# Soft experts on one Trainium2 core: a third shift of the logits on TensorE, and the end of the stage reordered

## The reference, cut to what matters

```python
# x: 8 x 256 tokens, d = 128; n = 64 experts, p = 32 slots each (2048 slots)
logits = (einsum('tzd,ed->tze', x, phi_w) + phi_b).reshape(t, z, n, p)
D = softmax(logits, axis=3)            # over the slots of an expert
C = softmax(logits, axis=2)            # over the experts of a slot
X = clip(einsum('tznp,tzd->npd', D, x), -33000.0, 65000.0)
X = tanh((X - mean(X)) * rsqrt(var(X) + eps))
Y = einsum('npd,ndH->npH', X, expert_w) + expert_b
out = einsum('tznp,npH->tzH', C, Y)
```

## Time and profile before

| | us |
|---|---|
| median of 3 runs | 3192.12 (3189.71 to 3195.6) |
| the profiled execution | 3195.53 |
| its span, first to last instruction | 3193.8 |
| PE, DVE, ACT, POOL busy in the span | 91%, 68%, 52%, 35% |
| mean granted clock of PE | 0.882 |

### The profile page before, as it was taken

How to read it: one execution, slowest core, us unless ns; L and a number is a source line. 1 busy time by engine, 2 the same in 40 slices (tenths; PEclk the granted TensorE clock), 3 DMA queues, 4 the chain that set the end, 5 groups by cost and what they waited for, 6 DMA issues and landing times. The chain is left out here.

```text
span 3193.8 us, 59125 instructions
## 1 busy us (share of the span) xinstructions
PE 2901.8 (91%) x22942; PEld 1673.4 (52%) x22949; DVE 2175.2 (68%) x4849; ACT 1645.8 (52%) x3323; POOL 1120.1 (35%) x532
## 2 busy tenths in 40 slices
PE   8888899998999999898968898888889899998998
PEld 3333344343899999643444454444453344574547
DVE  5777635556677777767588886877861559926991
ACT  3554543443333333336466776776753557725761
POOL 1111130002100000100088787877840219912990
PEclk8999999999555555699979998999999899999999
DMA  5344323022000000030532222222202001250224
GB/s 155 93 103 105 90 83 113 7 88 87 4 4 4 4 4 4 2 109 13 199 100 88 80 90 80 87 84 80 90 27 99 5 1 79 93 198 1 93 107 183
DMA packets 113495, 234.37 MB, mean 73 GB/s; under 512 B 13760, under 2 KB 50752, under 8 KB 104768
## 3 DMA queue, kind: packets, MB, share of 16 engines
q1 hardware_dynamic: 113216, 230.59, 22.3%
HBM read 185.71 MB, written 44.83 MB: 72 GB/s over the span
## 5 line engine op out<-in xcount | busy, mean ns | idle before, releaser
L2723 DVE TENSOR_TENSOR_SCAN s_hh<-psum,s_dbu 128x512 f32<-128x512 f32 x384 | 447.3, 1206 | 76.0 <-ACT psum L2335 75.9
L1447 PE MATMUL psum<-h_ring,h_parts 128*128 128x4 f16 x12264 | 478.0, 168 | 0.6 <-DVE h_ring L1590 0.4
L2593 POOL TENSOR_TENSOR s_dbu<-s_du,s_bb 128x1024 f32<-128x1024 f32 x191 | 447.1, 2360 | 67.0 <-DVE s_hh L2723 56.3
L1447 PEld LDWEIGHTS psum<-h_ring,h_parts 128*128 128x128 f16 x12264 | 429.5, 106 | 48.8 <-DVE h_ring L1590 0.9
L1509 ACT ACTIVATE h_now<-psum 128x16 f32<-128x16 f32 x1024 | 188.4, 184 | 324.3 <-PE psum L1447 317.8
L2335 ACT ACTIVATE psum<-s_delta,s_decay 128x512 f32<-128x512 f32 x384 | 256.5, 685 | 108.4 <-DVE s_hh L2723 106.3
L2227 PEld LDWEIGHTS psum<-w_c,s_term 128*128 128x128 f32 x1536 | 202.2, 151 | 136.6 <-issue 117.4
L1590 DVE TENSOR_SCALAR h_ring<-h_now 128x16 f16<-128x16 f32 x1024 | 179.6, 175 | 116.3 <-ACT h_now L1509 4.5
L1000 POOL MEMSET r_weights<- 128x512 f32 x4 | 2.1, 526 | 721.2 <-POOLq L1399 512.0
L2227 PE MATMUL psum<-w_c,s_term 128*128 128x128 f32 x1536 | 234.4, 290 | 9.1 <-ACT s_y L2413 8.6
L1592 DVE SCALAR_TENSOR_TENSOR h_ring<-h_now,h_ring 128x16 f16<-128x16 f32 x1024 | 180.0, 176 | 35.2
(11 more groups left out here) (583 smaller groups left out, 6218.1 us busy)
## 6 DMA issues: line engine op xcount, KB each, us to landing
s_bb<-s_wide SPq DMA_DIRECT2D x192, 256.0 KB, 3.4
x_spill<-x_flip SPq DMA_DIRECT2D x28, 1024.0 KB, 3.8
f_share<-f_wide SPq DMA_DIRECT2D x208, 128.0 KB, 3.0
s_cc<-s_wide SPq DMA_DIRECT2D x60, 256.0 KB, 3.4
a_ks<-a_spread SPq DMA_DIRECT2D x96, 128.0 KB, 3.3
a_qs<-a_spread SPq DMA_DIRECT2D x96, 128.0 KB, 3.9
x_spare<-x_spill SPq DMA_DIRECT2D x4, 2048.0 KB, 7.7
x_raw<-x_spill SPq DMA_DIRECT2D x4, 2048.0 KB, 7.7
```

Of the source, the lines that this page charges most:

```text
L1447: mm = nc.tensor.matmul(here[:, cols], parts[:, part, GROUP * grp + p, :], ring[:, (i - 1) % RING, grp, cut, cols], start=False, stop=True ...
L2593: nc.gpsimd.tensor_tensor(dbu[:, s % D_RING], du[:, t % 2], both(bb[:, s % B_RING, :]), ALU.mult).then_inc(dbu_ready, 1)
L2723: nc.vector.tensor_tensor_scan(hh[:, s % 4, half, :], DECAYS[i % 3], dbu[:, s % D_RING, half, :], 0.0, ALU.mult, ALU.add).then_inc(scan_do ...
```

## The change

It does five things in `soft_experts`.

1. `shift(n, 3)` is added on PE, behind the first transposes of the round; `lower(n, 3)` goes from DVE, and ACT's exponential of quarter 3 reads PSUM (`raise_shifted`) instead of SBUF. `logits(n+1, 2)` waits for that exponential.
2. For tile 15 the division is split: DVE divides quarters 0 and 1 (`first_shares`), POOL quarters 2 and 3, each with an increment of its own, and each `add_tile` waits for its own quarter.
3. Tile 14's transposes go from behind `of_expert` to between the `add_tile` of tile 15, through bank 7 alone; tile 15's go behind all the experts' matmuls.
4. Each mean waits for its own clipped quarter. ACT takes squares 2 and 3 between the logarithms and exponentials, and `raise_across(15)` comes behind the copies of tile 14. Only the expert bank that shares a bank with a variance waits for a logarithm.
5. Units 0 to 6 are now tiles 0 to 13 from device memory and unit 7 is tiles 14 and 15; the outputs turn through banks 1 to 3.

```diff
             SUMS = 3
+            DVE_PARTS = 2
-            MEAN, VAR, Y, OUT = (0, 1, 2, 3), (4, 5, 6, 0), (1, 2, 3, 0), (4, 5, 6)
+            MEAN, VAR, Y, OUT = (0, 1, 2, 3), (4, 5, 6, 0), (1, 2, 3, 0), (1, 2, 3)
-                return bank[LATE[q]] if n >= TILES - 2 else TURN
+                return bank[LATE[q]] if n >= TILES - 1 else TURN
...
                             if c == 3:
-                                pe.wait_ge(lowered, 2 * n + 1)
-                            elif c == 2:
-                                pe.wait_ge(lowered, 2 * n)
+                                pe.wait_ge(lowered, n + 1)
...
-                        pe.wait_ge(share_ready, n + 1)
+                        if n < TILES - 1:
+                            pe.wait_ge(share_ready, n + 1)
+                        elif c < DVE_PARTS:
+                            pe.wait_ge(first_shares, c + 1)
+                        else:
+                            pe.wait_ge(share_ready, n + c - DVE_PARTS + 1)
...
                             flip_part(n - 2, q)
+                            if q == 0:
+                                shift(n, 3)
...
                     for c in range(PARTS):
+                        flip_part(TILES - 2, c)
                         add_tile(TILES - 1, c)
                     pe.wait_ge(raw_kept, TILES * PARTS)
+                    for j in range(PARTS):
+                        pe.wait_ge(bounded, j + 1)
+                        nc.tensor.matmul(bank[MEAN[j]], g.mean_of, fixed_(z, j), start=True, stop=True).then_inc(mean_ready, 1)
...
-                    pe.wait_ge(logged, PARTS)
                     for j in range(PARTS):
+                        if Y[j] in VAR:
+                            pe.wait_ge(logged, VAR.index(Y[j]) + 1)
...
-                    for q in range(PARTS):
-                        flip_part(TILES - 2, q)
                     for j in range(PARTS):
-                        if j == 2:
-                            for q in range(PARTS):
-                                flip_part(TILES - 1, q)
...
+                    for q in range(PARTS):
+                        flip_part(TILES - 1, q)
...
-                        raise_e(n, 3)
+                        raise_shifted(n, 3)
...
                     for q in range(PARTS):
                         keep_flip(TILES - 2, q)
+                    raise_across(TILES - 1)
+                    square(0)
+                    square(1)
+                    for j in range(PARTS):
+                        invert(j)
+                        if j + 2 < PARTS:
+                            square(j + 2)
...
-                    divide(TILES - 1)
+                    pool.wait_ge(inv_ready, TILES)
+                    for c in range(DVE_PARTS, PARTS):
+                        e = by_expert(part(TILES - 1, c))
+                        nc.gpsimd.tensor_tensor(e, e, over_slots(total[:, (TILES - 1) % 2, c * PE_:(c + 1) * PE_]),
+                                                ALU.mult).then_inc(share_ready, 1)
...
-                        lower(n, 3)
...
                     total_of(TILES - 1)
+                    dve.wait_ge(inv_ready, TILES)
+                    for c in range(DVE_PARTS):
+                        e = by_expert(part(TILES - 1, c))
+                        nc.vector.tensor_tensor(e, e, total[:, (TILES - 1) % 2, c * PE_:(c + 1) * PE_].unsqueeze(2).broadcast_to([P, PE_, SLOT]),
+                                                ALU.mult).then_inc(first_shares, 1)
```

More of the change, by code:

```diff
@@ L3390, in _ @@
                         mm.then_inc(y_ready, 1)
+                    for q in range(PARTS):
+                        flip_part(TILES - 1, q)
                     for u in range(UNITS):
-                        if u == 0:
+                        if u < UNITS - 1:
+                            pe.wait_ge(fetched[u % 4], (u // 4 + 1) * 16)
+                        else:
                             pe.wait_ge(flip_kept, TILES * PARTS)
-                        else:
-                            pe.wait_ge(fetched[(u - 1) % 4], ((u - 1) // 4 + 1) * 16)
                         if u >= 3:
@@ L3464, in _, with square, invert @@
                             keep(n + 1, 3)
-                    raise_across(TILES - 1)
-                    for j in range(PARTS):
+                    def square(j):
                         act.wait_ge(centred, j + 1)
                         nc.scalar.activation(fixed_(rstd, j), fixed_(z, j), ACT.Square).then_inc(squared, 1)
-                    for j in range(PARTS):
+                    def invert(j):
                         act.wait_ge(var_ready, j + 1)
                         nc.scalar.activation(fixed_(rstd, j), bank[VAR[j]], ACT.Ln, bias=g.eps5).then_inc(logged, 1)
-                    for j in range(PARTS):
                         act.wait_ge(logged, j + 1)
@@ L3480, in _ @@
                     for j in range(PARTS):
-                        if j == 2:
-                            for q in range(PARTS):
-                                keep_flip(TILES - 1, q)
                         act.wait_ge(y_ready, j + 1)
                         nc.scalar.copy(yt[:, 4 * j:4 * j + 4, :].rearrange("p i h -> p (i h)"), bank[Y[j]]).then_inc(y_kept, 1)
+                    for q in range(PARTS):
+                        keep_flip(TILES - 1, q)
                 @block.gpsimd
@@ L3489, in over_slots @@
                     def over_slots(x):
[L3490 removed]
+                        return x.unsqueeze(2).broadcast_to([P, x.shape[1], SLOT])
                     def over_experts(x):
@@ L3592, in _ @@
                         dve.wait_ge(weighed, u + 1)
-                        first = (u - 1) * UNIT if u else TILES - UNIT
+                        first = u * UNIT
                         at = slice(first * P, first * P + WIDTH)
@@ L3603, in _ @@
                         sp.wait_ge(there, (TILES - UNIT) // 2 * 16)
-                    for u in range(1, UNITS):
-                        if u == 1:
+                    for u in range(UNITS - 1):
+                        if u == 0:
                             sp.wait_ge(added, TILES * PARTS)
+                        elif u == 1:
+                            sp.wait_ge(across_ready, TILES)
                         elif u == 2:
-                            sp.wait_ge(across_ready, TILES)
+                            sp.wait_ge(flipped, TILES * PARTS)
                         elif u == 3:
-                            sp.wait_ge(flipped, TILES * PARTS)
-                        elif u == 4:
                             sp.wait_ge(y_ready, PARTS)
@@ L3614, in _ @@
                             sp.wait_ge(weighed, u - 3)
-                        first = (u - 1) * UNIT
-                        sp.dma_start(homes[(u - 1) % 4], spill[first:first + UNIT].rearrange("u p f -> p u f")).then_inc(fetched[(u - 1) % 4], 16)
+                        first = u * UNIT
+                        sp.dma_start(homes[u % 4], spill[first:first + UNIT].rearrange("u p f -> p u f")).then_inc(fetched[u % 4], 16)
 def columns(v):
```

18 lines of the change are left out of this document (7 added, 11 removed).

## The result

Over 18 runs of each kernel the changed one takes 3203.56 us (3194.61 to 3210.38), the one before 3194.24 (3188.08 to 3202.74). The ratio is 1.0028, 95% interval 1.002 to 1.0036: slower by 9.3 us (6.4 to 11.5), where 6.9 was forecast. The profiled execution took 3206.41, its span is 3204.7.

The account below looks back on a forecast made before the run. DVE led, but PE was nearly full, with a floor of 11.20 in an 11.36 round. Per stage +8.9 (loop) - 4.8 (end) = +4.1, with 1.3 off once for the clock: +6.9, so 3199.0 us against 3192.12; range 3193.0 to 3204.5.

Parts of the forecast that it names:

- What bounds the kernel: Tile loop: DVE leads without a gap, POOL 0.44 behind, PE nearly full with a floor of 11.20 and 0.16 of waiting.
- The round grows by 0.70: Steady loop rounds: the third shift on PE lengthens each by 0.70, 12 x 0.70 = 8.4 us per stage.
- mostly taken up there: First rounds: three extra shifts, 2.57, vanish in PE's waits for DVE, all but 0.5.
- The end gives 4.8: End of a stage, from the last round's first shift T: weighing starts at 33.7 instead of 38.51, 4.8 earlier.
- The interleaving loses 2.1: Variances at the stage's end: ACT's new order of squares and logarithms makes PE wait 1.3 and 0.9, losing 2.1.
- Tanh [...] just hidden: Before the experts' matmuls: table load and tanh(0) done by T + 27.8, before PE at 27.95; otherwise some tenths lost.
- The split of the division costs nothing: Tile 15's division: DVE and POOL together take 3.2 instead of POOL's 3.65; no cost, as PE comes later.
- The clock, -1.3 once: First stage's experts' matmuls: shorter PE gaps avoid the lower 1.2 GHz clock level, taking 1.3 off once.
- The absolute time: Whole kernel's median: 3199.0 us against 3192.12, +0.22%, range 3193.0 to 3204.5.
- PE has headroom: Rival, tile loop: round falls to POOL's 10.91, the change makes the kernel faster, 3170.6 us; chance 0.06.
- The end gains all its waits: Rival, stage's end: weighing after 29.2 of PE work without waits, -0.4 per stage, about 3190 us; chance 0.14.
- The second softmax of tile 15 gets in the way: Rival, stage's end: `raise_across(15)` on ACT ends 4 later and delays the squares, +8 in all, 3207 us; chance 0.08.

Follow-up runs that it names:

- e8: Changed kernel without the third shift on PE and nothing in its place, so quarter 3's maxima are not taken off; 3171.17 us, 0.9945 of before.
- e3: Changed kernel with all four squares ahead of the first logarithm on ACT; 3202.94 us, 1.0025 of before.
- e4: Changed kernel with POOL dividing all of tile 15 in one instruction again; 3202.71 us, 1.0029 of before.
- e1: Kernel before with the loop's part of the change alone (shift of quarter 3 added, lowering removed); 3214.36 us, 1.0068 of before.
- e5: Changed kernel with one more DVE reduction per round, whose result nobody reads; 3202.33 us, 1.0032 of before.
- e9: Kernel before with the loop's part of the change alone, timed once more; 3213.38 us, 1.0063 of before.

## Why the prediction was right, and where its sizes were off

**What bounds the kernel.** "PE's own floor is 11.20: it is nearly full too" held: e8 gives 11.22. Reading start to start carried this. DVE's timeline without a gap had pointed at DVE, and DVE did lead, but by no more than 0.13.

**The round grows by 0.70.** It grew by 0.727 (12.08 against 11.353), 8.72 in twelve rounds instead of 8.4. The shift costs its 0.86; the wait that goes is 0.13, not the 0.16 that a sum of rounded starts had left. The first rounds took 0.75 instead of 0.5: of 2.57 added, "mostly taken up there" was right. With them the loop costs 9.47 instead of 8.9.

**The end gives 4.8.** It gave 4.75, and nearly each step stands where it was put. From T, forecast and measured: `add_tile` of tile 14 from 6.25, measured 6.40; tile 15's last sums done at 15.2, measured 15.32; variances from 18.6 and 18.75; PE's waits in them 1.3 and 0.9 against 1.10 and 0.63; `of_expert` 24.2 and 24.55; experts' matmuls 27.95 and 28.31; weighing 33.7 and 33.76. The last steps took 0.2 less than forecast (3.63 and 1.82 instead of 3.76 and 1.9, and 27.95 + 3.76 is 31.7, not 31.8), which made up for most of the late start. Bank 7's copy did set the pace of tile 15, 1.40 per quarter (3119.84, 3121.24, 3122.63, 3124.03): each group of transposes starts 0.14 after ACT's copy of the one before ended.

**The interleaving loses 2.1.** On PE's variances, yes (2.27 in e3), but only 1.06 of it can be had back by that edit: "Tanh [...] just hidden" means that whatever comes earlier than this meets tanh. The sum didn't need it, a plan for the next change does.

**The split of the division costs nothing.** It gains 0.2 (e4). DVE and POOL did get in each other's way. DVE's and POOL's timelines at that place, changed kernel:

```profile
3116.33 2.15 DVE L3595 TENSOR_TENSOR x_share<-x_share,x_total 128x512 f32<-128x512 f32 x2
```
```profile
3116.38 3.01 POOL L3533 TENSOR_TENSOR x_share<-x_share,x_total 128x512 f32<-128x512 f32 x2 [0.52 <-DVE x_total L3575]
```

The two DVE multiplications would take about 1.3 alone (L3590's median is 0.68), and the two POOL ones half of 3.66; together they end 3.06 after the first began, as if one after the other. That agrees with the exclusive lock of the Trainium skill's "SBUF — State Buffer", Who interferes with whom, and with the forecast's 3.2.

**The clock, -1.3 once.** This is the weakest term. In the two profiled executions it came: the first stage grew by 3.38 and the second by 4.72, 1.34 more. The new end held 1.00 in both stages of all its ten profiles, the old one lost 1.34, 1.6 and 4.4 in one stage of the two. But I had taken one drop, seen in one execution, as something that happens in each. If it did, the kernels with the new end would lie 1.3 lower against before than twice their stage's difference. Over the ten of them the two agree to 0.0 on average, single ones to -4.2 and +2.2. That speaks against 1.3 in the mean of runs and doesn't exclude it: the interval of the result, 6.4 to 11.5, holds +8.1 as well as +9.4. Of the 2.4 missed between +6.9 and +9.3, 1.2 are the sizes of loop and end (+4.72 per stage where +4.1 was forecast), and the rest is of the size of this term and of the noise.

**The absolute time.** Forecast was 3199.0, measured 3203.56, 0.9 under the upper end of the range. Of the 4.6 between them 2.4 are the change and 2.1 the kernel before, whose median over 18 runs is 3194.24 and not the 3192.12 of three. The mechanism and its price held; that the absolute time stayed in the range is in part luck.

**The rivals.** *PE has headroom* fell: with 0.86 more for PE per round and 0.61 less for DVE the round got longer (e1), DVE's work can be put back for nothing (e5), and the floor is 11.22 (e8), not 10.9. The rule behind it, the Trainium skill's "Perfetto Trace Analysis", Identifying the Most-Contended Engine, would take PE's weight-load share as one of two measures of its load; here that was 6.27 of 12.08, while taking out a single f32 matmul of 512 columns shortened the round by its whole 0.86 (e8, 11.22). For these rounds the runs contradict that measure, and the measurement decides. The page's other measure, MFU, the share of the peak arithmetic, neither the prediction nor a run worked out, so the rival tested half of the page's rule. *The end gains all its waits* fell: 4.6 are left between the weighing at 33.76 and the 29.2 of work without a wait. *The second softmax of tile 15 gets in the way* came close, as ACT's timeline of the changed kernel shows:

```profile
3124.71 1.91 ACT L3434 ACTIVATE x_raw<-x_raw 128x2048 f32<-128x2048 f32 x1
3126.67 0.63 ACT L3472 ACTIVATE x_share<-x_share 128x512 f32<-128x512 f32 x1
```

`raise_across(15)` ends at T + 17.05 and the first square starts right behind it, where I had put the end at 16.7 and the decision at 17. DVE had the first centred quarter ready at 3126.64, 0.02 after `raise_across(15)` ended, so it cost nothing and had nothing to spare.

**The DMAs** brought nothing late: no wait stands in front of any line of the weighing, and from its start to the end of the span it is 61.4 us in both kernels.

## What to carry to other kernels

When several engines are nearly full, find each one's floor by adding start-to-start times without the waits before moving work between them: here 0.61 taken from the engine that led was worth 0.13, and the 0.86 given to the next one cost all but that. A change of several parts should be split by experiment even if its sum is near zero, since one part may gain what the other loses: the old loop with the new end, the squares first and the transposes moved into the new wait is 0.43 to 0.48% faster than before, where the whole change is 0.28% slower. In a chain of waits, the gain of removing one is what lies between it and the next late thing (2.27 won, 1.06 kept).

## What the runs showed of the hardware beyond what was expected

- DVE's multiplication with both inputs in SBUF was held until a POOL instruction beside it had ended, 3.93, longer than the 2.92 at most of before. Line L3608 of DVE in the changed kernel, least, median and most in ns, against a POOL instruction of 4.14 us that ran at the same time:

```profile
L3608 DVE TENSOR_TENSOR x_share<-x_share x8: 627/678/3929, 2822.0 to 3137.0; 128x512 f32<-128x512 f32 x8
```
```profile
3131.88 4.14 POOL L3520 TENSOR_TENSOR x_norm<-x_raw,x_total 128x2048 f32<-128x2048 f32 x1 [7.50 <-DVE x_total L3561]
```

- PE's granted clock fell at places with idle stretches of 0.78 (e9) or 2.76 us (before, e1) in some executions and not in others of the same instructions: e1's and e9's first stages are the same kernel and the same waits, one is 220.44 long, the other 224.81. The new ends, with waits of up to 1.14 (e3), kept 1.00 in all twenty stages. A drop seen in one profile should be taken as a chance, not as a term.
- Apart from such drops a stage of 217 us repeats to about 0.05 us between stages, executions and chips, while whole executions of one kernel spread over 10 us and more. A difference of 0.2 us per stage, like e4's, can be read from a profile and from nothing else.
